# Moving a group's score broadcast and sum into its own step, in the attention stage of a graph-attention and expert kernel

## The chip, the core and the metric

The kernel runs on one core of a Trainium2 chip. The metric is the device time of one execution in microseconds (us), the median of several runs. One execution was also recorded by the hardware profiler; all rows below are from that execution.

## The reference

There are 128 graphs of 128 nodes with 256 features. Everything is float32. Cut to what matters:

```python
def gnn(h, adj, W, a):                       # h = layernorm(x)
    Wh = einsum('bnd,df->bnf', h, W)
    s1 = Wh @ a[:256, 0];  s2 = Wh @ a[256:, 0]
    e = s1[:, :, None] + s2[:, None, :]
    e = where(e > 0, e, 0.2 * e) + log(adj + 1e-6)
    return einsum('bij,bjf->bif', softmax(e, axis=-1), Wh)

x = x + gnn(layernorm(x), adj, W, a)
x = x + ffn(layernorm(x), ...)   # 8 experts, three 256x256 products each, two batch norms,
                                 # gates from a softmax of the mean over graphs
```

## The kernel before

The program has two parts. The first, about 335 of the 2493 us, is the attention stage, and only this one is touched. The second, the experts, needs the gates, which need the mean over all graphs, so it starts when the first part is over.

The attention stage takes the graphs in 32 groups of 4. It is a pipeline written out by hand: each engine has its own program, a function `step(g, layer)` that `over_groups` calls for g = -2 to 33, and an engine handles several groups in one step. In step g TensorE (PE) handles group g (projection), group g-2 (attention output) and group g+1 (transposes of its normalised rows). ScalarE (ACT), VectorE (DVE) and GpSimd (POOL) do likewise. Nothing but semaphores ties the engines together. Within an engine the order is that of the code, so an instruction that waits holds up everything behind it. Steps 6 to 21 also load and split the first weights of the experts (`layer == 1`), steps 22 to 29 the second (`layer == 2`); they run in loops.

The names, with the line of the profile for each, for group g:

- `x_sb` (L327, load by SyncE, SP), two buffers: the load for group g+2 waits until group g has been normalised. `st1`, `mv1` (DVE L572, L586): its statistics. `rstd1`, `nb1` (POOL L404, L407).
- `xn` (ACT L501, `normalise`): the normalised rows, one buffer. `ps_xT` (PE L782) and `xnT` (ACT L554): their transposes in PSUM and in SBUF, one buffer each.
- `ps_wide` (PE L731, `project`): `xnT` times `gw`, 258 columns: the projected rows and the two score columns. `wh` (ACT L550): their copy, two buffers by the parity of g. The copy of group g waits for `h_ready` of group g-2, whose product reads the same buffer.
- `ps_s` (PE L750): the second score of each node, broadcast over the partitions. `s_sb` (ACT L518): the sum with the first score. `l_sb` (DVE L611): the leaky slope. `neg_m` (DVE L616): minus the row maximum. `e_sb` (ACT L529): the exponential. `p_sb` (DVE L680): times `adj` + 1e-6. `rowsum` (DVE L687).
- `ps_pT` (PE L743), `pT` (ACT L511): the transpose of `p_sb`. `ps_h` (PE L769): `pT` times `wh`. It lies in the same banks as `ps_xT` (both are called `ps_th` in the profile). `x1` (DVE L665, called `h` or `w_bc` there): `ps_h` / rowsum + x.
- `acc` (DVE L636 for the lower half of a group, POOL L449 and L453 for the upper, called `resb`): the sum over graphs. `wq_hi` and `w_hi` (ACT L541, L545), `wq_lo` and `w_lo` (POOL L471, L476): the split of the experts' weights.

In the code `a` is group g-1, `b` group g-2, `nxt` group g+1 (on DVE and POOL group g+2), `t` group g-3 and `h` group g-4. `wait(eng, sem, n)` waits for n signals and does nothing for n <= 0; a group signals each of its semaphores once.

Of the kernel before, what the change touches and what calls it, by code (L numbers as in the profile page):

```python
# [21 lines left out]
ACT = mybir.ActivationFunctionType  # L22
AX_X = mybir.AxisListType.X

P = 128
# [6 lines left out]
def wait(eng, sem, value):  # L32

    if isinstance(value, int) and value <= 0:
        return
    eng.wait_ge(sem, value)


def adj_ffn(nc, x, adj, gnn_w, gnn_a, wr, br, w1, b1, g1, be1, m1, v1, w2, b2, g2, be2, m2, v2, wo, bo, out):
    B, N, D = x.shape  # L40
    E = wr.shape[1]
    C = D // P
    GB = 4
    T = GB * N
    G = B // GB
# [11 lines left out]
    with ExitStack() as ctx:  # L57
# [7 lines left out]
        ident = sb("ident", [P, P])  # L65
# [12 lines left out]
        mean_all = sb("mean_all", [P, G, GB])  # L78
# [106 lines left out]
        with ExitStack() as sa:  # L185
# [24 lines left out]
            xnT = sba("xnT", [P, C, T])  # L210
# [77 lines left out]
            def num(g):  # L288
                return 2 * g[0] + g[1]

            def ago(g, n):

                q = g[1] - n
                return (g[0] + q // 2, q % 2)

            def exists(g):
                return not isinstance(g[0], int) or 0 <= num(g) < G
# [12 lines left out]
            def is_step(g, n):  # L310

                return isinstance(g[0], int) and num(g) == n
# [172 lines left out]
            @block.scalar  # L485
            def _(act):

                act.wait_ge(proj_T, 1)
                nc.scalar.activation(gwT[:, :, :], ps_h[:, 0:C, :], ACT.Copy)
                nc.scalar.activation(a_cols[:, :], ps_s[:, 0, 0:2 * C], ACT.Copy).then_inc(proj_T_copied, 1)  # L490
                act.wait_ge(va_ready, 1)
                nc.scalar.activation(gw[:, :, D:D + 2], ps_s[:, 1, 0:2 * C].rearrange("p (c k) -> p c k", k=2),
                                     ACT.Copy).then_inc(va_copied, 1)

                def normalise(g):

                    p = g[1]
                    act.wait_ge(nb1_done, num(g) + 1)
                    wait(act, xnT_ready, num(g))
                    for b4 in range(GB):  # L500
                        last = nc.scalar.activation(xn[:, b4, :], x_sb[p][:, b4, :], ACT.Identity,  # L501
                                                    bias=nb1[p][:, b4:b4 + 1], scale=rstd1[p][:, b4:b4 + 1])
                    last.then_inc(xn_done, 1)

                def step(g, layer):
                    p = g[1]
                    b = ago(g, 2)
                    if exists(b):
                        act.wait_ge(pT_ready, num(b) + 1)
                        wait(act, h_ready, num(b))  # L510
                        nc.scalar.activation(pT[:, :, :], ps_pT[:, :, :], ACT.Copy).then_inc(pT_copied, 1)  # L511
                    a = ago(g, 1)
                    if exists(a):
                        r = a[1]
                        act.wait_ge(s2b_ready, num(a) + 1)
                        wait(act, l_done, num(a))
                        for b4 in range(GB):
                            last = nc.scalar.activation(s_sb[:, b4, :], ps_s[:, b4, :], ACT.Identity,  # L518
                                                        bias=wh[r][:, b4, D:D + 1])
                        last.then_inc(s_done, 1)  # L520
                    nxt = ago(g, -1)
                    if exists(nxt):
                        normalise(nxt)
                    if exists(a):
                        act.wait_ge(neg_m_done, num(a) + 1)
                        wait(act, p_done, num(a))

                        for b4 in range(GB):
                            last = nc.scalar.activation(e_sb[:, b4, :], l_sb[:, b4, :], ACT.Exp,  # L529
                                                        bias=neg_m[:, b4:b4 + 1])  # L530
                        last.then_inc(e_done, 1)
                    if is_step(g, BN_STEP - 1):
                        act.wait_ge(bn_T, 1)
                        nc.scalar.activation(bn_in[:, :, :, :].rearrange("p l i k -> p (l i) k"), ps_bn,
                                             ACT.Copy).then_inc(bn_copied, 1)
                    if is_step(g, G):
                        tile_copy(act, 0, ps_x0)
                    if layer == 1 and p == 1:
                        e = g[0] - K0
                        act.wait_ge(wq_sum, 4 * (e + 1))  # L540
                        nc.scalar.activation(wq_hi[:, e, :, :], w_stage[:, 0:Q, :], ACT.Copy).then_inc(wq_hi_done, 1)  # L541
                    if layer == 2:
                        i = second(g)
                        act.wait_ge(w2_loaded[p], 16 * (g[0] - K1 + 1))
                        nc.scalar.activation(w_hi[:, i, :, :].rearrange("p c n -> p (c n)"),  # L545
                                             w_half[p], ACT.Copy).then_inc(w_hi_done, 1)
                    if exists(g):
                        act.wait_ge(wh_ready, num(g) + 1)
                        wait(act, h_ready, num(g) - 1)
                        nc.scalar.activation(wh[p][:, :, :], ps_wide[:, :, 0:D + 2], ACT.Copy).then_inc(wh_copied, 1)  # L550
                    if exists(nxt):
                        act.wait_ge(xnT_ready, num(nxt) + 1)
                        wait(act, wh_ready, num(nxt))
                        nc.scalar.activation(xnT[:, :, :], ps_xT, ACT.Copy).then_inc(xnT_copied, 1)  # L554
                    t = ago(g, 3)
                    if exists(t) and not is_step(t, G - 1):
                        act.wait_ge(stats2_done, num(t) + 1)
                        nc.scalar.activation(mean_all[:, num(t), :], mv2[t[1]][:, :, 0],
                                             ACT.Copy).then_inc(mean2_done, 1)

                over_groups(act, step)
                for group in range(3):
                    tile_high(act, 0, group)

            @block.vector
            def _(dve):
# [27 lines left out]
                def step(g, layer):  # L594
# [5 lines left out]
                    def stats_part(b4):  # L600

                        if exists(nxt):
                            stats_1(nxt, b4)

                    if exists(a):

                        stats_part(0)
                        stats_part(1)
                        dve.wait_ge(s_done, num(a) + 1)
                        wait(dve, e_done, num(a))  # L610
                        nc.vector.scalar_tensor_tensor(out=l_sb[:, :, :], in0=s_sb[:, :, :], scalar=SLOPE,  # L611
                                                       in1=s_sb[:, :, :], op0=ALU.mult,
                                                       op1=ALU.max).then_inc(l_done, 1)
                        stats_part(2)
                        dve.wait_ge(l_done, num(a) + 1)
                        nc.vector.tensor_reduce(neg_m[:, :], l_sb[:, :, :], AX_X, ALU.max,  # L616
                                                negate=True).then_inc(neg_m_done, 1)
                        stats_part(3)
                    else:
                        for b4 in range(GB):  # L620
                            stats_part(b4)
# [88 lines left out]
            def _(pe):  # L710
# [22 lines left out]
                    return mm  # L733

                def step(g, layer):
                    a = ago(g, 1)
                    b = ago(g, 2)
                    nxt = ago(g, -1)
                    if exists(b):
# [2 lines left out]
                        for b4 in range(GB):  # L742
                            last = nc.tensor.transpose(ps_pT[:, b4, :], p_sb[:, b4, :], ident[:, :])  # L743
                        last.then_inc(pT_ready, 1)
                    if exists(a):

                        pe.wait_ge(wh_copied, num(a) + 1)
                        wait(pe, s_done, num(a))
                        for b4 in range(GB):
                            last = nc.tensor.matmul(ps_s[:, b4, :], wh[a[1]][:, b4, D + 1:D + 2].to_broadcast([P, P]),  # L750
                                                    ident[:, :], start=True, stop=True)
                        last.then_inc(s2b_ready, 1)
                    if is_step(g, G):
                        pe.wait_ge(wh_copied, G)
                        tile_transpose(pe, 0, ps_x0)
# [2 lines left out]
                    if exists(g):  # L758
                        pe.wait_ge(xnT_copied, num(g) + 1)
                        wait(pe, wh_copied, num(g))  # L760
                        project(g, range(GB // 2))
                    if exists(b):

                        pe.wait_ge(pT_copied, num(b) + 1)
# [7 lines left out]
                                last.then_inc(h_low_ready, 1)  # L772
                        last.then_inc(h_ready, 1)
                    if exists(g):
                        project(g, range(GB // 2, GB)).then_inc(wh_ready, 1)
                    if exists(nxt):
                        pe.wait_ge(xn_done, num(nxt) + 1)
                        wait(pe, xnT_copied, num(nxt))
# [507 lines left out]
```

## Time and profile before

| | us |
|---|---|
| time, median of 3 runs | 2492.35 (2492.15 to 2494.12) |
| time of the profiled execution | 2494.85 |
| its span | 2493.1 |
| attention stage | about 0 to 335 |
| first product of the experts' part starts | 348.92 |
| TensorE busy, whole span | 2409.5 (97%) |
| VectorE busy | 1728.2 (69%) |
| ScalarE busy | 1643.7 (66%) |
| GpSimd busy | 458.9 (18%) |

The shares are means over two stages with different limits. The slices of the page show it: TensorE reads 7 and 8 tenths in the first five slices (62 us each) and 9 in all that follow. The chain that ended last lies on TensorE for 85% of the span, on lines of the experts' part. "Idle before" is how long an engine stood still before an instruction, and behind the arrow stands what ended it.

### The profile page before, as it was taken

Reading aid. Unit: us, or ns where it says so; the run is one execution under the profiler, and the core shown is the slowest. Engines: PE = TensorE matmul, PEld = TensorE weight load, DVE = VectorE, ACT = ScalarE, POOL = GpSimd, SP = SyncE. Lnnn points to the kernel's source line nnn. Section 1 sums busy time; section 2 is a strip of 40 time slices with the busy share of each in tenths; the row PEclk is TensorE's granted clock in tenths of the full one; section 3 lists DMA queues with packets and bytes.
Section 4 is the critical chain, followed back from the end, with each engine's and each line's share of the span. In section 5 each row is a group of like instructions: output and inputs, shape, how many; then the busy total and the mean of one; then the engine's idle time right before and its main releaser. Section 6 shows DMA issues by size and latency. Waiting matters only on the chain.

```text
span 2493.1 us, 45081 instructions
## 1 busy us (share of the span) xinstructions
PE 2409.5 (97%) x16304; PEld 2217.6 (89%) x16304; DVE 1728.2 (69%) x2444; ACT 1643.7 (66%) x2497; POOL 458.9 (18%) x487
## 2 busy tenths in 40 slices
PE   7888869999999999999999999999999999999999
PEld 6767658999999999999999999999999999999998
DVE  6888866666666666666666666666666666666665
ACT  6777746666666666666666666666666666666665
POOL 4666632111111100110111111111111100110110
PEclk9999979999999999999999999999999999999999
DMA  5666620000000000000000000000000000000000
GB/s 183 199 189 195 206 89 26 27 26 25 25 25 25 25 25 25 25 17 25 17 17 25 25 25 25 25 25 25 25 25 25 25 25 25 25 17 19 15 17 26
DMA packets 91178, 116.16 MB, mean 47 GB/s; under 512 B 4700, under 2 KB 78856, under 8 KB 91144
## 3 DMA queue, kind: packets, MB, share of 16 engines
q1 hardware_dynamic: 91144, 115.73, 14.4%
q8 instruction: 19, 0.31, 0.1%
q14 instruction: 15, 0.12, 0.0%
HBM read 82.16 MB, written 33.55 MB: 46 GB/s over the span
## 4 chain that ended last, share of the span: by engine, by line
PE 85%; DVE 1%; ACT 0%; issue 0%; ACTq 0%; DVEq 0%
PE ps_y L1186 29%; PE ps_wide L171 29%; PE ps_wide L1168 26%; PE ps_t L132 1%; DVE h_lo L1073 0%; PE ps_y L1234 0%; DVE h L1080 0%; DVE z L1066 0%; ACT h_hi L975 0%; DVE feat_sum L1106 0%; DVE x1t L124 0%; ACT v L980 0%; DVE resb L179 0%; DVE z L1056 0%; DVE h_lo L1088 0%
## 5 line engine op out<-in xcount | busy, mean ns | idle before, releaser
L980 ACT ACTIVATE v<-ps_wide,bn_cols 128x256 f32<-128x256 f32 x768 | 434.7, 566 | 398.6 <-PE ps_wide L1168 271.5
L988 ACT ACTIVATE h<-ps_wide,bn_cols 128x512 f32<-128x512 f32 x512 | 399.2, 780 | 327.2 <-PE ps_wide L171 327.2
L1186 PE MATMUL ps_y<-wo_lo,h_hi 128*128 128x256 f32 x2048 | 578.8, 283 | 0.0
L1186 PE MATMUL ps_y<-wo_hi,h_hi 128*128 128x256 f32 x2048 | 577.2, 282 | 1.6 <-DVE h_lo L1088 1.6
L1186 PE MATMUL ps_y<-wo_hi,h_lo 128*128 128x256 f32 x2048 | 578.3, 282 | 0.0
L1168 PE MATMUL ps_wide<-xq_hi,wq_hi 128*128 128x256 f32 x1792 | 505.6, 282 | 13.8 <-PEq L185 8.4
L1168 PE MATMUL ps_wide<-xq_lo,wq_hi 128*128 128x256 f32 x1792 | 509.2, 284 | 0.0
L1168 PE MATMUL ps_wide<-xq_hi,wq_lo 128*128 128x256 f32 x1792 | 506.5, 283 | 0.0
L1088 DVE TENSOR_TENSOR h_lo<-h,h_hi 128x1024 fp32r<-128x1024 f32 x256 | 318.3, 1243 | 241.9 <-ACT h_hi L994 241.9
L1066 DVE SCALAR_TENSOR_TENSOR z<-ps_wide,bn_cols,v 128x512 f32<-128x512 f32 x256 | 192.2, 751 | 318.2 <-PE ps_wide L1168 318.2
L171 PE MATMUL ps_wide<-h_hi,w_hi 128*128 128x512 f32 x1024 | 404.2, 395 | 2.1 <-DVE h_lo L1073 2.1
L171 PE MATMUL ps_wide<-h_lo,w_hi 128*128 128x512 f32 x1024 | 405.7, 396 | 0.0
L171 PE MATMUL ps_wide<-h_hi,w_lo 128*128 128x512 f32 x1024 | 405.4, 396 | 0.0
L1073 DVE SCALAR_TENSOR_TENSOR h_lo<-z,h_hi 128x1024 fp32r<-128x1024 f32 x256 | 315.8, 1234 | 117.4 <-ACT h_hi L975 117.4
L1186 PEld LDWEIGHTS ps_y<-wo_hi,h_hi 128*128 128x128 f32 x2048 | 386.5, 189 | 1.9 <-DVE h_lo L1088 1.8
L1186 PEld LDWEIGHTS ps_y<-wo_hi,h_lo 128*128 128x128 f32 x2048 | 387.4, 189 | 0.0
L1186 PEld LDWEIGHTS ps_y<-wo_lo,h_hi 128*128 128x128 f32 x2048 | 386.5, 189 | 0.1
L958 POOL TENSOR_TENSOR resb<-resb,bias_out 128x1024 f32<-128x1024 f32 x32 | 85.9, 2685 | 1534.3 <-DMA resb<-x_scratch 1534.3
L1168 PEld LDWEIGHTS ps_wide<-xq_hi,wq_hi 128*128 128x128 f32 x1792 | 340.7, 190 | 26.7 <-issue 9.4
L1168 PEld LDWEIGHTS ps_wide<-xq_hi,wq_lo 128*128 128x128 f32 x1792 | 338.0, 189 | 10.0
L1168 PEld LDWEIGHTS ps_wide<-xq_lo,wq_hi 128*128 128x128 f32 x1792 | 339.5, 189 | 0.0
L1080 DVE TENSOR_TENSOR h<-h,w_bc 128x1024 f32<-128x1024 f32 x256 | 313.8, 1226 | 7.8 <-ACT w_bc L1022 4.9
(131 smaller groups left out, 3141.5 us busy)
## 6 DMA issues: line engine op xcount, KB each, us to landing
x_sb<-in_x SPq DMA_DIRECT2D x32, 512.0 KB, 3.5
res<-in_x SPq DMA_DIRECT2D x32, 512.0 KB, 4.5
x1t<-x_scratch SPq DMA_DIRECT2D x32, 512.0 KB, 3.2
resb<-x_scratch SPq DMA_DIRECT2D x32, 512.0 KB, 3.3
out<-resb SPq DMA_DIRECT2D x32, 512.0 KB, 3.0
adj_sb<-in_adj SPq DMA_DIRECT2D x32, 256.0 KB, 4.7
x_scratch<-h SPq DMA_DIRECT2D x16, 512.0 KB, 3.2
x_scratch<-w_bc SPq DMA_DIRECT2D x16, 512.0 KB, 3.1
```

What stands on the lines that cost most here:

```text
L132: last = nc.tensor.transpose(ps_x[:, c, b4 * N:(b4 + 1) * N], x1t[:, b4, c * P:(c + 1) * P], ident[:, :])
L171: mm = nc.tensor.matmul(acc_ps, w[:, i, c, cols], s[:, c, :], start=start and n == 0, stop=stop and n == len(terms) - 1)
L958: nc.gpsimd.tensor_tensor(resb[:, :, :], resb[:, :, :], bias_out[:, None, :].to_broadcast([P, GB, D]), ALU.add).then_inc(resb_done, 1)
L980: nc.scalar.activation(v[:, slot, :], ps_l1[:, 0, 0:H], ACT.Identity, bias=bn_cols[:, 1, cols], scale=bn_cols[:, 0, cols]).then_inc(done, 1)
L988: nc.scalar.activation(h2[:, m, :], ps_l2[:, m, :], ACT.Relu, bias=bn_cols[:, 3, cols], scale=bn_cols[:, 2, cols]).then_inc(r2_done, 1)
L1066: nc.vector.scalar_tensor_tensor(out=z[:, 0, :], in0=ps_l1[:, 1, :], scalar=bn_cols[:, 0, C * e:C * e + 1], in1=v[:, 0:2, :].rearrange("p ...
L1073: nc.vector.scalar_tensor_tensor(out=h1_lo[:, :, :], in0=z[:, :, :], scalar=0.0, in1=h1_hi[:, :, :].bitcast(F32), op0=ALU.max, op1=ALU.sub ...
L1080: nc.vector.tensor_tensor(h2w[:, :, :].rearrange("p c (b n) -> p (c b) n", n=N), h2[:, :, :].rearrange("p c (b n) -> p (c b) n", n=N), w_b ...
L1088: nc.vector.tensor_tensor(h2_lo[p][:, :, :], h2w[:, :, :], h2_hi[p][:, :, :].bitcast(F32), ALU.subtract).then_inc(lo2_done, 1)
L1168: mm = nc.tensor.matmul(out_ps, w[:, e, q, :], x[:, q, :], start=start and n == 0, stop=stop and n == len(terms) - 1, skip_group_check=True)
L1186: mm = nc.tensor.matmul(ps_y[:, b4, :], h[:, c, cols], w[:, e, c, :], start=(e == 0 and k == 0 and b4 % per_bank == 0), stop=(e == E - 1 a ...
```

## The change

On TensorE `ps_s` is computed for group g at the end of its own step, behind the attention output of group g-2, where it was computed one step later, behind the transposes of `p_sb`. The projection is issued in one piece of all four graphs, where it was issued in two halves around the attention output. On ScalarE `s_sb` is computed for group g in its own step too, behind the next group's `normalise`; the exponential and the copy of the projected rows `wh` now stand ahead of `normalise`, and the weights' split behind the copy of the transposes `xnT`. On VectorE one of the four statistics instructions that stood ahead of `l_sb` and one of those behind it move down by a place. No instruction is added or removed; GpSimd's and SyncE's code is the same.

```diff
@@ ScalarE, step(g, layer)
                     a = ago(g, 1)
                     if exists(a):
-                        r = a[1]
-                        act.wait_ge(s2b_ready, num(a) + 1)
-                        wait(act, l_done, num(a))
-                        for b4 in range(GB):
-                            last = nc.scalar.activation(s_sb[:, b4, :], ps_s[:, b4, :], ACT.Identity,
-                                                        bias=wh[r][:, b4, D:D + 1])
-                        last.then_inc(s_done, 1)
-                    nxt = ago(g, -1)
-                    if exists(nxt):
-                        normalise(nxt)
-                    if exists(a):
                         act.wait_ge(neg_m_done, num(a) + 1)
                         wait(act, p_done, num(a))
...
                         last.then_inc(e_done, 1)
+                    if exists(g):
+                        act.wait_ge(wh_ready, num(g) + 1)
+                        wait(act, h_ready, num(g) - 1)
+                        nc.scalar.activation(wh[p][:, :, :], ps_wide[:, :, 0:D + 2], ACT.Copy).then_inc(wh_copied, 1)
+                    nxt = ago(g, -1)
+                    if exists(nxt):
+                        normalise(nxt)
+                    if exists(g):
+                        act.wait_ge(s2b_ready, num(g) + 1)
+                        wait(act, l_done, num(g))
+                        for b4 in range(GB):
+                            last = nc.scalar.activation(s_sb[:, b4, :], ps_s[:, b4, :], ACT.Identity,
+                                                        bias=wh[p][:, b4, D:D + 1])
+                        last.then_inc(s_done, 1)
...
+                    if exists(nxt):
+                        act.wait_ge(xnT_ready, num(nxt) + 1)
+                        wait(act, wh_ready, num(nxt))
+                        nc.scalar.activation(xnT[:, :, :], ps_xT, ACT.Copy).then_inc(xnT_copied, 1)
+                    t = ago(g, 3)
+                    if exists(t) and not is_step(t, G - 1):
+                        act.wait_ge(stats2_done, num(t) + 1)
...
                         nc.scalar.activation(w_hi[:, i, :, :].rearrange("p c n -> p (c n)"),
                                              w_half[p], ACT.Copy).then_inc(w_hi_done, 1)
-                    if exists(g):
-                        act.wait_ge(wh_ready, num(g) + 1)
-                        wait(act, h_ready, num(g) - 1)
...
-                    if exists(nxt):
-                        act.wait_ge(xnT_ready, num(nxt) + 1)
-                        wait(act, wh_ready, num(nxt))
...
@@ VectorE, step(g, layer)
                         stats_part(0)
-                        stats_part(1)
                         dve.wait_ge(s_done, num(a) + 1)
                         wait(dve, e_done, num(a))
...
-                        stats_part(2)
+                        stats_part(1)
                         dve.wait_ge(l_done, num(a) + 1)
                         nc.vector.tensor_reduce(neg_m[:, :], l_sb[:, :, :], AX_X, ALU.max,
                                                 negate=True).then_inc(neg_m_done, 1)
+                        stats_part(2)
                         stats_part(3)
@@ TensorE, step(g, layer)
                         last.then_inc(pT_ready, 1)
-                    if exists(a):
-
-                        pe.wait_ge(wh_copied, num(a) + 1)
-                        wait(pe, s_done, num(a))
-                        for b4 in range(GB):
-                            last = nc.tensor.matmul(ps_s[:, b4, :], wh[a[1]][:, b4, D + 1:D + 2].to_broadcast([P, P]),
-                                                    ident[:, :], start=True, stop=True)
-                        last.then_inc(s2b_ready, 1)
...
                         wait(pe, wh_copied, num(g))
-                        project(g, range(GB // 2))
+                        project(g, range(GB)).then_inc(wh_ready, 1)
                     if exists(b):
...
                         last.then_inc(h_ready, 1)
                     if exists(g):
-                        project(g, range(GB // 2, GB)).then_inc(wh_ready, 1)
+
+                        pe.wait_ge(wh_copied, num(g) + 1)
+                        wait(pe, s_done, num(g))
+                        for b4 in range(GB):
+                            last = nc.tensor.matmul(ps_s[:, b4, :], wh[g[1]][:, b4, D + 1:D + 2].to_broadcast([P, P]),
+                                                    ident[:, :], start=True, stop=True)
+                        last.then_inc(s2b_ready, 1)
```

TensorE's order in one step inside the loops, with what each instruction waits for, before:

```order
90 L743 MATMUL ps_pT<-ident,p_sb 128x128 [waits pT_copied,p_done]
92 L750 MATMUL ps_s<-ident,wh 128x128 [waits s_done,wh_copied]
94 L731 MATMUL ps_wide<-gw,xnT 128x258 [waits wh_copied,xnT_copied]
95 L731 MATMUL ps_wide<-gw,xnT 128x258 x3
96 L769 MATMUL ps_th<-wh,pT 128x256 [waits x1_done,xnT_copied,wh_copied,pT_copied]
98 L731 MATMUL ps_wide<-gw,xnT 128x258 x4
```

The same step after the change:

```order
87 L741 MATMUL ps_pT<-ident,p_sb 128x128 [waits pT_copied,p_done]
89 L730 MATMUL ps_wide<-gw,xnT 128x258 [waits wh_copied,xnT_copied]
90 L730 MATMUL ps_wide<-gw,xnT 128x258 x7
91 L759 MATMUL ps_th<-wh,pT 128x256 [waits x1_done,xnT_copied,wh_copied,pT_copied]
93 L769 MATMUL ps_s<-ident,wh 128x128 [waits s_done,wh_copied]
96 L778 MATMUL ps_th<-ident,xn 128x128 [waits x1_low_done,xnT_copied,xn_done]
```

The transposes of the next group (`ps_th<-ident,xn`) now stand behind `ps_s`, which waits for `wh_copied` of the same step.

ScalarE's order in a step of the second loop (`layer == 2`), before:

```order
116 L511 ACTIVATE pT<-ps_pT 128x512 [waits h_ready,pT_ready]
117 L518 ACTIVATE s_sb<-ps_s,wh 128x128 [waits l_done,s2b_ready]
120 L501 ACTIVATE xn<-x_sb,nb_0,rstd_0 128x256 [waits xnT_ready,nb1_done]
122 L529 ACTIVATE e_sb<-l_sb,neg_m 128x128 [waits p_done,neg_m_done]
125 L545 ACTIVATE w_hi<-w_stage 128x512
126 L550 ACTIVATE wh<-ps_wide 128x1032 [waits h_ready,wh_ready]
127 L554 ACTIVATE xnT<-ps_th 128x1024 [waits wh_ready,xnT_ready]
```

The same step after the change:

```order
118 L511 ACTIVATE pT<-ps_pT 128x512 [waits h_ready,pT_ready]
119 L518 ACTIVATE e_sb<-l_sb,neg_m 128x128 [waits p_done,neg_m_done]
121 L524 ACTIVATE wh<-ps_wide 128x1032 [waits h_ready,wh_ready]
123 L501 ACTIVATE xn<-x_sb,nb_0,rstd_0 128x256 [waits xnT_ready,nb1_done]
125 L532 ACTIVATE s_sb<-ps_s,wh 128x128 [waits l_done,s2b_ready]
127 L542 ACTIVATE xnT<-ps_th 128x1024 [waits wh_ready,xnT_ready]
131 L557 ACTIVATE w_hi<-w_stage 128x512
```

`normalise` (`xn`) moved from ahead of the exponential and of `wh` to behind both.

## Rows read from the trace of the kernel before

**Rows 1.** Windows: stretch; length; busy of PE, PEld, DVE, ACT, POOL; PEclk, DMA, GB/s
```profile
0.00:62.00 62.00, 49.33 (x258) 41.78 (x259) 38.03 (x130) 41.28 (x91) 27.69 (x56) 1.00 0.59 182
62.00:125.00 63.00, 53.96 (x285) 44.71 (x284) 55.89 (x170) 46.98 (x104) 43.63 (x68) 0.95 0.65 199
...
187.00:249.00 62.00, 52.62 (x268) 43.58 (x267) 54.94 (x164) 44.99 (x101) 42.19 (x62) 0.92 0.63 195
```

**Rows 2.** Waits, 60 to 310 us: who waited for whom, us in total, times, longest
```profile
ACT xnT L554 <- PE ps_th L782: 28.4, 24, 2.3
DVE l_sb L611 <- ACT s_sb L518: 24.8, 24, 2.0
```

**Rows 3.** Line L611 alone: ns min/median/max, and what its engine waited for before it
```profile
L611 DVE SCALAR_TENSOR_TENSOR l_sb<-s_sb x32: 691/886/2477, 25.6 to 329.3; 128x512 f32<-128x512 f32 x32
...
  ACT s_sb L518: 34.7, 32
```

**Rows 4.** Timeline, two steps inside the first loop: start, us, engine, line, operation
```profile
199.96 2.08 ACT L501 ACTIVATE xn<-x_sb,nb,rstd 128x256 f32<-128x256 f32 x4
...
202.06 1.28 ACT L529 ACTIVATE e_sb<-l_sb,neg_m 128x128 f32<-128x128 f32 x4
202.22 0.37 SPq L327 DMA_DIRECT2D x_sb<-in_x  x1
...
203.25 0.93 ACT L541 ACTIVATE wq_hi<-w_stage 128x896 f32 x1
...
205.65 1.01 POOL L443 TENSOR_TENSOR rstd_all<-ve,minus_half 128x4 f32 x1 [0.18 <-POOL ve L440]
205.78 0.67 DVE L680 SCALAR_TENSOR_TENSOR p_sb<-adj_sb,e_sb 128x512 f32<-128x512 f32 x1
...
207.90 1.91 PE L731 MATMUL ps_wide<-gw,xnT 128*128 128x258 f32 x8
...
209.19 2.10 POOL L471 TENSOR_TENSOR wq_lo<-w_stage,wq_hi 128x896 f32 x1
209.36 2.47 DVE L611 SCALAR_TENSOR_TENSOR l_sb<-s_sb 128x512 f32<-128x512 f32 x1 [0.67 <-ACT s_sb L518]
...
209.64 1.89 PE L769 MATMUL ps_th<-wh,pT 128*128 128x256 f32 x8
...
211.37 1.90 PE L731 MATMUL ps_wide<-gw,xnT 128*128 128x258 f32 x8
```

**Rows 5.** Timeline, the first steps of the stage
```profile
9.35 2.06 ACT L501 ACTIVATE xn<-x_sb,nb,rstd 128x256 f32<-128x256 f32 x4
...
11.46 1.97 PE L782 MATMUL ps_th<-ident,xn 128*128 128x128 f32 x8 [2.22 <-ACT xn L501]
...
14.84 1.02 ACT L554 ACTIVATE xnT<-ps_th 128x1024 f32<-128x1024 f32 x1
...
16.00 6.13 PE L731 MATMUL ps_wide<-gw,xnT 128*128 128x258 f32 x16 [1.40 <-ACT xnT L554]
...
22.18 1.03 ACT L550 ACTIVATE wh<-ps_wide 128x1032 f32<-128x1032 f32 x1 [4.36 <-PE ps_wide L731]
23.10 1.02 ACT L554 ACTIVATE xnT<-ps_th 128x1024 f32<-128x1024 f32 x1
...
24.25 3.67 PE L731 MATMUL ps_wide<-gw,xnT 128*128 128x258 f32 x16
...
26.24 0.42 DVE L572 BATCH_NORM_STATS2 st<-x_sb 128x6 f32<-128x256 f32 x1
26.57 0.67 DVE L616 TENSOR_REDUCE neg_m<-l_sb 128x4 f32<-128x512 f32 x1
...
27.77 1.03 PE L782 MATMUL ps_th<-ident,xn 128*128 128x128 f32 x8
```

**Rows 6.** Timeline, the projection of the last group
```profile
318.18 1.91 PE L731 MATMUL ps_wide<-gw,xnT 128*128 128x258 f32 x8
```

**Rows 7.** Tile x_sb: from issue to landing of its 32 loads
```profile
DMA to landing us min/median/max: 3.4/3.5/4.9
```

More of the change, by code:

```diff
@@ L535, in step @@
                                              ACT.Copy).then_inc(bn_copied, 1)
+                    if exists(nxt):
[5 more added lines that the diff above has]
+                        act.wait_ge(stats2_done, num(t) + 1)
+                        nc.scalar.activation(mean_all[:, num(t), :], mv2[t[1]][:, :, 0],
+                                             ACT.Copy).then_inc(mean2_done, 1)
                     if is_step(g, G):
@@ L546, in step @@
                                              w_half[p], ACT.Copy).then_inc(w_hi_done, 1)
-                    if exists(g):
-                        act.wait_ge(wh_ready, num(g) + 1)
-                        wait(act, h_ready, num(g) - 1)
-                        nc.scalar.activation(wh[p][:, :, :], ps_wide[:, :, 0:D + 2], ACT.Copy).then_inc(wh_copied, 1)
-                    if exists(nxt):
-                        act.wait_ge(xnT_ready, num(nxt) + 1)
-                        wait(act, wh_ready, num(nxt))
[L554 to L559, printed above, removed]
                 over_groups(act, step)
@@ L735, in step @@
                 def step(g, layer):
-                    a = ago(g, 1)
                     b = ago(g, 2)
```

## The prediction

> **What bounds the kernel now.** I read the page first, for which part of the span the change touches: the attention stage, the first 335 of 2493.1 us. There TensorE is busy 7 and 8 tenths, behind it 9, so the shares over the whole span say nothing about this stage. Then the windows of the stage [rows 1]. No engine is full: in 187 to 249 us VectorE is busy 54.94 of 62 us, TensorE 52.62, ScalarE 44.99. TensorE's clock is granted at 1.00 in the first 62 us and at 0.95 and 0.92 later, so it is at the lower of its two levels for 10 to 16% of that time. A stage in which two engines are nearly full and none is full is set by rounds: a chain that leaves an engine and comes back to it one step later. The waits [rows 2] show the round of now. VectorE stands before `l_sb` until `s_sb` is there, 24.8 us in 24 steps; over the whole stage 34.7 us in 32 [rows 3], 1.08 us a step. ScalarE waits longer, 28.4 us in 24 steps, for the transposes behind `xnT`, but it has slack: it is busy 45 of 62 us. So VectorE's order sets the end of a step: it works, and stands only from `p_sb` over two products of TensorE and the sum on ScalarE to `l_sb`.
>
> A step's length comes from the projection of group 1 at 24.25 [rows 5] and of group 31 at 318.18 [rows 6]: 293.93 us in 30 steps, 9.80 us each.
>
> **The change, part by part.** No instruction is added or dropped, so the busy times stay, about, and only rounds move. The durations are from rows 4 and 5.
>
> *The wait of VectorE before `l_sb`.* The sum is now formed one step earlier. This wait goes, worth up to 34.7 us if nothing else is late.
>
> *The new round.* The projection is in one piece, so its signal `wh_ready` comes when all four graphs are through. Behind it TensorE does the attention output `ps_h` of group g-2. The copy `wh` of group g waits for both, since `ps_h` reads the buffer that the copy overwrites. That wait was there before, but the second half of the projection stood behind `ps_h` and covered it. `normalise` is now queued behind this copy on ScalarE, the transposes of the next group wait for `normalise`, the copy `xnT` for the transposes, and the next projection for that copy. Each link waits for the one before, and the last starts the first. In numbers, at the full clock:
> - projection, 16 rows of the profile: eight start-to-start are 209.64 - 207.90 = 1.74, so 3.48 [rows 4]
> - `ps_h` to its end: 1.89 [rows 4]
> - TensorE to ScalarE: 16.00 + 6.13 = 22.13 to 22.18, 0.05 [rows 5]
> - `wh` to the start of what follows it: 23.10 - 22.18 = 0.92 [rows 5]
> - `normalise`: 2.08 [rows 4]
> - ScalarE to TensorE: 9.35 + 2.06 = 11.41 to 11.46, 0.05 [rows 5]
> - transposes: 1.03, the row at 27.77 [rows 5]
> - to ScalarE: 0.05, and `xnT` 1.02 [rows 5]
> - `xnT` to the projection: 14.84 + 1.02 = 15.86 to 16.00, 0.14 [rows 5]
>
> Sum 10.71 us, against 9.80. `ps_s` lies beside `normalise`, `s_sb` beside the transposes (2.08 against about 1.1 of TensorE, then 1.14 of ScalarE, as long as the transposes): free but for 0.1. The transposes of `p_sb` lie beside `xnT`. In 30 steps: 30 x 0.91 = +27.3 us. VectorE's work, 54.94 of 62 us or some 9 us a step, fits into 10.71; the removed wait turns into waiting elsewhere, and the gain is nothing.
>
> *The start.* Before, `wh` of group 0 at 22.18 was followed by `xnT` of group 1 at 23.10 and its projection at 24.25. Now behind `wh`, at 23.10, come `normalise` (2.08), the transposes (1.03), `xnT` (1.02) and three hops (0.24): 27.47. That is +3.2 us.
>
> *The clock.* The 9.80 holds its share at the lower level, the 10.71 none. At 10 to 16% of some 340 us, 35 to 54 us lie at the lower level. TensorE's part of the round is 3.48 + 1.89 + 1.03 = 6.4 of 10.71, 60%, and runs at half speed there, so that a us at that level loses 0.3 us: 10 to 16. But the level fell behind pauses of TensorE, and the new round has several short pauses (about 1 us before `ps_s`, 1 before the transposes, 1 before the projection) in place of a long one. Bounds: 0 (it never falls) to +16. I take +8.
>
> *The loads of `x_sb`.* SyncE issues the load of group g+2 when `normalise` of group g is done. That is later now, and VectorE's first statistics instruction in a step, ahead of `l_sb`, needs this load. This is a second round: end of `normalise` to issue 202.22 - 202.04 = 0.18 [rows 4]; landing 3.5 [rows 7]; statistics 26.57 - 26.24 = 0.33 [rows 5]; `l_sb` 0.69 [rows 3]; statistics 0.33; `neg_m` 0.67 [rows 5]; exponential 203.25 - 202.06 = 1.19 [rows 4]; `wh` 0.92; `normalise` 2.08: 9.9, with hops about 10.0. It stays 0.7 below the first round, which is little. In the first loop SyncE also issues two weight loads ahead of every second load of x, and `l_sb` may be held (below), so I add 2 us, between 0 and +9.
>
> *`l_sb` beside GpSimd.* At 209.36 it took 2.47 us where its shortest is 0.691: it started 0.17 after `wq_lo` on GpSimd, 2.10 long, and ended 0.54 after it [rows 3, 4]. It now comes at another place of GpSimd's order, behind `acc`'s upper half and near the weights' split. Held by the same instruction it costs up to 1.8 us in the second round, 0.7 of it covered. The Trainium skill has a rule here (SBUF — State Buffer, section "SBUF: two separate sides"): a VectorE operation with two SBUF inputs and a GpSimd operation that reads SBUF exclude each other for the whole instruction, and the one that starts second waits. The trace agrees for `l_sb` beside `wq_lo` and not for `p_sb`: at 205.78 it ran 0.13 behind the start of a 1.01 us operation of GpSimd on four elements and took 0.67 [rows 4]. By the rule `p_sb` could be up to 0.9 longer where it meets that operation; by the row nothing, and the sum goes by the row.
>
> *The rest.* The weights' split now stands ahead of `pT`: 0.93 us at most [rows 4], under the 3.48 of the projection that precedes `ps_h`. The exponential ahead of `wh` starts when `neg_m` is done, and queued behind it are `wh`, `normalise` and all of the first round: that is the second round, priced above. The statistics that moved on VectorE: zero.
>
> *Sum*, against the profiled execution's 2494.85 (span 2493.1): +27.3 + 3.2 + 8 + 2 = +40.5, so 2535.3. That execution lies 2.5 above the median of 2492.35; the median afterwards should be about 2533.
>
> **The rivals.**
> 1. *VectorE stays the bound, and its wait is simply gone (faster).* For it: 34.7 us of wait [rows 3], and VectorE the fullest engine. Against it: the new round. It decides from the point where the copy `wh` need not wait for `ps_h`: the round is then 10.71 - 1.89 = 8.8, and VectorE's step 9.80 - 1.08 = 8.7. Time: 2492.35 - 30 x 1.0 = about 2462. I give 4%, since the wait on `h_ready` stands in the code with the value of the same step.
> 2. *The load of x ends last.* For it: only 0.7 us of slack, the store, the `res` and the `adj` loads are now issued right behind it, and landings of up to 4.9 were seen [rows 7]. Against it: the load is first in the queue. At 4.9 the round is 11.4, +21 us over the forecast; with `l_sb` held in eight steps instead, +9. Time 2542 to 2554, say 2549. 12%.
> 3. *The clock falls far more often.* If 40% of the stage lay at the lower level: 340 x 0.4 x 0.3 = 41 in place of 8. Time 2566. For it: TensorE idles a fifth of each round now. Against: the pauses are short. 6%.
> 4. *No change.* The round would have to shorten by 0.9 a step, through an overlap that I don't see. Time 2492. 3%.
>
> **How the numbers follow.** The forecast, 2533, gets 75%. Its own range: low with the clock and the loads at nothing, and the round 0.15 shorter, 2492 + 27 + 3 - 5 = 2517; high with both at their upper bound, 2548. Rival 2 lies mostly inside up to 2553. Out of the range are left rivals 1, 3, 4 and the tail of 2, some 15%. Range 2516 to 2553. By over 0.2% (5 us, what a measurement here can tell from no change): faster 4%, within 3%, slower 93%.
>
> **What would show it.** Right: steps of 10.5 to 11 us, the same length throughout the stage; no wait of `l_sb` for `s_sb`; before `wh` ScalarE waits for `ps_h`, not for the projection; TensorE waits before `ps_s` for `wh`, before the transposes for `xn` and before the projection for `xnT`; the experts' part starts some 40 us later and is as long as before. `l_sb`'s first release by the load of x in most steps would speak for rival 2, a granted clock under 0.9 in the windows for rival 3. Wrong: steps under 10 us, or VectorE without pauses.

## The result and the profile after

| | before | after |
|---|---|---|
| time, median of 5 runs | 2492.35 us (2491.86 to 2494.12) | 2536.80 us (2536.0 to 2537.45) |
| span of the profiled execution, us | 2493.1 | 2535.5 |
| projection of group 1 starts | 24.25 | 27.95 |
| projection of group 31 starts | 318.18 | 361.52 |
| a step between them | 9.80 | 11.12 |
| experts' part starts | 348.92 | 390.19 |

The ratio is 1.0177, 95% interval [1.0163, 1.0191]: 44 us slower; 2533 was forecast. The span grew by 42.4 us: +3.7 at the start, 30 x 1.32 = +39.6 in the steps, -2.1 from the last projection to the experts' part and +1.1 in the experts' part, which is as long as before to 0.05%.

One step of the changed kernel, its timeline, as in [rows 4] (start, us, engine, line, operation; in brackets how long the engine stood and what ended it):

```profile
206.43 3.75 PE L730 MATMUL ps_wide<-gw,xnT 128*128 128x258 f32 x16 [0.68 <-ACT xnT L542]
...
208.39 0.43 DVE L571 BATCH_NORM_STATS2 st<-x_sb 128x6 f32<-128x256 f32 x1 [2.17 <-DMA x_sb<-in_x]
208.73 0.67 DVE L609 SCALAR_TENSOR_TENSOR l_sb<-s_sb 128x512 f32<-128x512 f32 x1
...
210.02 1.89 PE L759 MATMUL ps_th<-wh,pT 128*128 128x256 f32 x8
...
210.36 1.28 ACT L518 ACTIVATE e_sb<-l_sb,neg_m 128x128 f32<-128x128 f32 x4 [3.41 <-DVE neg_m L614]
...
212.01 1.03 ACT L524 ACTIVATE wh<-ps_wide 128x1032 f32<-128x1032 f32 x1 [0.36 <-PE ps_th L759]
...
212.93 2.06 ACT L501 ACTIVATE xn<-x_sb,nb,rstd 128x256 f32<-128x256 f32 x4
213.09 1.16 PE L769 MATMUL ps_s<-ident,wh 128*128 128x128 f32 x8 [1.18 <-ACT wh L524]
...
215.05 1.09 PE L778 MATMUL ps_th<-ident,xn 128*128 128x128 f32 x8 [0.80 <-ACT xn L501]
215.18 0.37 SPq L327 DMA_DIRECT2D x_sb<-in_x  x1
...
216.18 1.02 ACT L542 ACTIVATE xnT<-ps_th 128x1024 f32<-128x1024 f32 x1 [0.16 <-PE ps_th L778]
```

Read it as a ladder. The projection starts at 206.43; 3.59 later `ps_h`; 1.99 after that `wh` on ScalarE, released by `ps_h` (0.36 us of waiting); 0.92 later `normalise`; 2.12 later the transposes; 1.13 later `xnT`; and 1.07 after its start, at 217.25, the next projection. The sum is 10.82 us and the next projection starts 10.82 after the last. TensorE stands three times, 0.68, 1.18 and 0.80 us, and each time a ScalarE instruction of this ladder ends it.

This step is one of the shortest, and the steps are not all alike: 12 of the 30 take 10.76 to 10.87 us, the others up to 11.96. Two things lengthen them. In seven pairs of steps and the first one TensorE's clock falls to the lower level (below). And in eight steps of the first loop, every second one, GpSimd holds `l_sb`, the exponential ends later, and `wh` follows the exponential and not `ps_h`:

```profile
218.33 2.08 POOL L471 TENSOR_TENSOR wq_lo<-w_stage,wq_hi 128x896 f32 x1 [0.48 <-ACT wq_hi L553]
219.41 1.55 DVE L609 SCALAR_TENSOR_TENSOR l_sb<-s_sb 128x512 f32<-128x512 f32 x1
...
220.85 1.89 PE L759 MATMUL ps_th<-wh,pT 128*128 128x256 f32 x8
...
221.92 1.28 ACT L518 ACTIVATE e_sb<-l_sb,neg_m 128x128 f32<-128x128 f32 x4 [3.30 <-DVE neg_m L614]
...
223.10 1.00 ACT L524 ACTIVATE wh<-ps_wide 128x1032 f32<-128x1032 f32 x1
```

That step starts at 217.25, its `wh` 5.85 later in place of 5.58, and it is 11.09 long. Where the clock doesn't fall all such steps are 11.08 or 11.09.

The waits of 60 to 340 us, as in [rows 2]: who waited for whom, us in total, times, longest.

```profile
POOL ve L400 <- DVE mv L585: 86.8, 25, 7.1
ACT e_sb L518 <- DVE neg_m L614: 79.7, 25, 4.4
DVE st L571 <- DMA x_sb<-in_x: 64.4, 25, 4.2
...
PE ps_s L769 <- ACT wh L524: 30.7, 25, 1.4
...
PE ps_th L778 <- ACT xn L501: 20.1, 25, 0.8
PE ps_wide L730 <- ACT xnT L542: 14.7, 26, 0.7
ACT wh L524 <- PE ps_th L759: 9.8, 16, 1.4
```

`l_sb`, which waited 34.7 us for `s_sb` [rows 3], waits 0.5 us now, once:

```profile
L609 DVE SCALAR_TENSOR_TENSOR l_sb<-s_sb x32: 673/675/2389, 30.0 to 370.6; 128x512 f32<-128x512 f32 x32
...
  ACT s_sb L532: 0.5, 1
```

In its place VectorE waits for the load of x, 99.6 us in 32 steps, where it was 17.3 us in 5. And that load takes longer to land than in [rows 7]:

```profile
  DMA x_sb<-in_x: 99.6, 32
...
DMA to landing us min/median/max: 3.5/3.9/5.6
```

The three longest waits of the list are those of engines with slack. How little their length says shows in the load's 64.4 us: cutting its round alone won 5.5 us (below). The ladder's own waits are the short ones at the end.

### The profile page after: what moved, and what is told of

Same layout as the page of the kernel before. It is cut to its first block, busy times and chain, and to the rows that moved or that the text cites. A ratio compares the mean times of both kernels' runs of the same rounds, so it can differ in the third digit from the quotient of the medians.

```text
span 2535.5 us, 45093 instructions
## 1 busy us (share of the span) xinstructions
PE 2412.7 (95%) x16304; PEld 2218.3 (87%) x16304; DVE 1717.1 (68%) x2444; ACT 1638.9 (65%) x2497; POOL 459.4 (18%) x487
## 4 chain that ended last, share of the span: by engine, by line
PE 83%; DVE 1%; ACT 0%; issue 0%; ACTq 0%; DVEq 0%
PE ps_y L1182 29%; PE ps_wide L171 28%; PE ps_wide L1164 25%; PE ps_t L132 1%; DVE h_lo L1069 0%; DVE h L1076 0%; PE ps_y L1230 0%; DVE z L1062 0%; DVE x1t L124 0%; ACT h_hi L971 0%; DVE feat_sum L1102 0%; ACT v L976 0%; DVE resb L179 0%; DVE z L1052 0%; DVE h_lo L1084 0%
```

## The experiments

All times are medians of runs beside the kernel before on the same chip, in us. "Step" is the mean over the 30 steps between the projections of groups 1 and 31.

| kernel | us | ratio to before, 95% interval | step |
|---|---|---|---|
| before | 2492 to 2494 | | 9.80 |
| changed | 2536.8 | 1.0177 [1.0163, 1.0191] | 11.12 |
| projection in halves again | 2536.35 | 1.0173 [1.0156, 1.0190] | 11.08 |
| normalise ahead again | 2497.43 | 1.0017 [1.0007, 1.0026] | 9.88 |
| wh doesn't wait | 2519.52 | 1.0101 [1.0084, 1.0118] | 10.53 |
| first statistics behind l_sb | 2531.28 | 1.0150 [1.0133, 1.0167] | 10.96 |
| both of these | 2490.58 | 0.9994 [0.9984, 1.0003] | 9.59 |
| wh doesn't wait, all statistics behind neg_m | 2477.72 | 0.9932 [0.9915, 0.9949] | 9.14 |
| before, projection in one piece | 2494.54 | 1.0004 [0.9995, 1.0014] | 9.85 |
| ps_s twice | 2531.69 | 1.0152 [1.0135, 1.0169] | 10.98 |
| reordered, one statistics ahead of l_sb | 2468.78 | 0.9899 [0.9882, 0.9915] | 8.96 |
| two ahead | 2463.26 | 0.9875 [0.9859, 0.9892] | 8.78 |
| three ahead | 2462.14 | 0.9870 [0.9853, 0.9886] | 8.81 |

**The projection in one piece.** It was undone in the changed kernel, and done alone in the kernel before.

```diff
-                        project(g, range(GB)).then_inc(wh_ready, 1)
+                        project(g, range(GB // 2))
...
+                        project(g, range(GB // 2, GB)).then_inc(wh_ready, 1)
```

> The changed kernel with the projection in two halves around the attention output again, all else as changed. Theory (the round: projection, attention output, copy wh, normalise, transposes, copy xnT): the same two pieces of TensorE work, 3.5 + 1.9 us, stand ahead of the copy wh in either order, so the step stays at 11.1 us and the time within 3 us of the changed kernel's 2536.8. Rival (the projection in one piece is what costs, since the attention output and with it VectorE's x1 come 1.7 us later): the step falls by up to 1.3 us to that of before, 2500.

> The kernel before with one part of the change: the projection in one piece, ahead of the attention output. Theory: wh is copied behind the attention output in either order, normalise and ps_s are where they were, so the round stays; x1's first half can start 1.7 us later, but VectorE reaches it later than that: within 4 us of the kernel before, 2493. Rival (the one piece costs): 10 us or more over the kernel before.

Measured: 2536.35 and 2494.54, both as the theory had it. This part of the change costs nothing that can be measured. In the changed kernel the order of the two pieces ahead of `wh` doesn't matter, only their sum.

**Normalise ahead of the exponential again.**

```diff
+                    nxt = ago(g, -1)
+                    if exists(nxt):
+                        normalise(nxt)
                     a = ago(g, 1)
                     if exists(a):
                         act.wait_ge(neg_m_done, num(a) + 1)
...
-                    nxt = ago(g, -1)
-                    if exists(nxt):
-                        normalise(nxt)
```

> The changed kernel with ScalarE's normalise put back ahead of the exponential, all else as changed. Theory: normalise leaves the round. What stays is projection 3.6, attention output 2.0 to its signal, wh 1.0, ps_s 1.15 (it stands ahead of the transposes), transposes 1.1, xnT 1.07 = 9.9 us against 10.83, and the load of x is issued 3 us earlier or more, so that its waits go too: a step of 9.8 to 10.0 against 11.12, so 2537 - 30 x 1.2 = 2501, range 2494 to 2508. Rival (the load of x ends last): it gains as much or more, 2485 to 2495, since the load's round is what normalise holds. Rival (one piece and the later x1 cost): no more than 10 us gained, 2527.

Measured: 2497.43, 39 us of the 44 back by this place alone. The step is 9.9 to 10.0 in every case but the first, as summed. In this run the clock stays at its upper level from group 1 to group 31, so the 39 us hold what the clock cost too. Here is what the round has become:

```profile
206.33 1.89 PE L759 MATMUL ps_th<-wh,pT 128*128 128x256 f32 x8
208.32 1.03 ACT L527 ACTIVATE wh<-ps_wide 128x1032 f32<-128x1032 f32 x1 [1.95 <-PE ps_th L759]
209.40 1.16 PE L769 MATMUL ps_s<-ident,wh 128*128 128x128 f32 x8 [1.18 <-ACT wh L527]
210.40 1.04 PE L778 MATMUL ps_th<-ident,xn 128*128 128x128 f32 x8
...
211.61 1.04 ACT L542 ACTIVATE xnT<-ps_th 128x1024 f32<-128x1024 f32 x1
...
212.71 3.75 PE L730 MATMUL ps_wide<-gw,xnT 128*128 128x258 f32 x16 [0.83 <-ACT xnT L542]
...
216.30 1.89 PE L759 MATMUL ps_th<-wh,pT 128*128 128x256 f32 x8
```

From `ps_h` to `ps_h` 9.97 us. The transposes now follow `ps_s` without a wait; `wh` still stands in the round, since `ps_s` needs it and is ahead of the transposes. The wait for the load of x fell from 99.6 us in 32 steps to 16.6 in 5. So `normalise` is in both rounds, that of the ladder and that of the load, and this run alone doesn't tell their shares.

**The two rounds apart.** First the wait of `wh` for `ps_h` was taken out. For this the attention output multiplies a constant tile in place of `wh`: the three kernels that do so leave the projected rows out of that product, so they don't compute the attention. They tell only what the wait costs. The edit:

```diff
                         act.wait_ge(wh_ready, num(g) + 1)
-                        wait(act, h_ready, num(g) - 1)
...
-                            last = nc.tensor.matmul(ps_h[:, b4, :], pT[:, b4, :], wh[b[1]][:, b4, 0:D], start=True,
+                            last = nc.tensor.matmul(ps_h[:, b4, :], pT[:, b4, :], gwT[:, b4 % C, :], start=True,
```

> The changed kernel, but the attention output multiplies pT with a constant tile (the projection's transposed weights) in place of the projected rows wh, so the copy wh no longer waits for it; the product has the same shape and place. Theory: the attention output's 1.9 us leave the first round, 10.83 - 1.9 = 8.9. The second round (end of normalise, issue and landing of the load of x, statistics, l_sb, neg_m, exponential, wh, normalise) is then the longest, 10.0 to 10.6 us: a step of 10.2 to 10.6 and 2537 - 30 x 0.7 = 2516, range 2509 to 2522. Rival (the second round has been the last one in most steps already): no gain, 2530 or more. Rival (neither round, VectorE's own order): 2480.

Then VectorE's `stats_part(0)` was put behind `l_sb`, one line moved:

> The changed kernel with VectorE's first statistics instruction of a step behind l_sb in place of ahead of it, so that l_sb doesn't wait for the load of x (neg_m stands behind it still, one statistics instruction later, as does the rest). Theory: the first round ends last in most steps, so little is gained: 0 to 6 us, 2533. Rival (the load of x ends last): neg_m still waits for the statistics, so the wait shortens by l_sb's 0.6 to 2.3 us; where the load ends last each step shortens by that, 20 us or more, 2517 or less.

Then both together, and last `stats_part(0)` to `(3)` all behind `neg_m`:

> The changed kernel with two edits: the attention output multiplies pT with a constant tile in place of wh (the copy wh no longer waits for it), and VectorE's first statistics instruction stands behind l_sb. Theory: both rounds are shortened, the first to 8.9 us and the second by l_sb and a statistics instruction to about 9.0 to 9.4; VectorE's own work is about 8.5 to 9. A step of 9.0 to 9.4, 2537 - 30 x 1.9 = 2480, range 2473 to 2492. Rival (the rounds are not what sets the step): no more than the single edits' sum.

> The changed kernel, with the attention output on a constant tile in place of wh (the copy wh doesn't wait for it) and all four statistics instructions of the next x behind neg_m. With one of them behind l_sb alone the step was 9.6 us and VectorE still waited for the load of x, 32.9 us in 25 steps. Theory: the load's round (normalise, load, statistics, neg_m, exponential, wh, normalise) is now cut, since neg_m no longer waits for the load; what stays is the first round without the attention output, 8.9, and VectorE's own order, 8.5 to 9.0. A step of 9.0 to 9.2, 2490.6 - 30 x 0.5 = 2475, range 2468 to 2481. Rival (something else held the step at 9.6): 2488 or more.

Measured: -17.3, -5.5, -46.2 and -59.1 us against the changed kernel's median (the kernel before lay between 2492.35 and 2494.2 beside these runs). Cutting the first round alone won 17, cutting the second alone 5.5, and both together 46, twice the single gains' sum. That is how two rounds of nearly the same length show themselves: each hides what the other would give. The first single edit leaves the second round last, at 10.2 to 10.6 in most steps, and at 11.08 in the first loop's steps with `l_sb` held, just what these steps take in the changed kernel. The second leaves the first at 10.8. A part of the 46 is the clock, which falls eight times in the changed kernel, four and six times in the single edits, and never with both. The third run was forecast at 2480 and came at 2490.6, inside its range but 0.4 us a step too long. The wait that is left is VectorE's for the load (60 to 310 us):

```profile
DVE st L570 <- DMA x_sb<-in_x: 32.9, 25, 1.5
```

The second round was still last: only `l_sb`'s 0.6 us had left it, where the expectation took off a statistics instruction too, which still stands ahead of `neg_m`. With all four statistics behind `neg_m` the same row reads

```profile
DVE st L570 <- DMA x_sb<-in_x: 3.8, 10, 1.1
```

and most steps are 9.04, their mean 9.14. With both rounds cut, the changed kernel is faster than the one before. That is no fair race, since it leaves out a product's input and with it a wait; the reordered version below shows the gain with nothing left out.

**The clock.** The granted clock has eight stretches at the lower level, 27 us in all, in the changed kernel between the projections of groups 1 and 31, and ten, 34 us, in the kernel before. The ten stretches that the next expectation gives the changed kernel are two too many. What they cost can be read from the lengths of the steps. The 30 steps are 333.57 us. At 10.82 each they would be 324.6; eight steps with `l_sb` held add some 2.1. The other 6.8 us, by difference, lie in the steps with a low stretch and in those right behind them, some 0.85 us a stretch. To test it, `ps_s` was computed twice, so that TensorE pauses less:

```diff
-                        for b4 in range(GB):
+                        for b4 in [*range(GB), *range(GB)]:
                             last = nc.tensor.matmul(ps_s[:, b4, :], wh[g[1]][:, b4, D + 1:D + 2].to_broadcast([P, P]),
```

> The changed kernel with ps_s computed twice in each step, in the 0.8 us in which TensorE waits for normalise (the second time over the first, the same values). It tells what the clock's lower level costs in the changed kernel, which has ten stretches at that level of 3.4 us each in the stage, behind the pauses of TensorE. Theory: the level falls less often or not at all, and the transposes start 0 to 0.2 us later in each step: with 0.8 us won a stretch, 2537 - 8 + 3 = 2532, range 2527 to 2538. Rival (the lower level costs nothing, since ScalarE sets the round): no gain, 2537 to 2542, whatever the clock does.

Measured: 2531.69, 5.1 us less with 128 matmuls more. Windows of the changed kernel and of this one (columns as in [rows 1]):

```profile
187.00:249.00 62.00, 47.33 (x240) 38.89 (x239) 49.80 (x156) 41.16 (x94) 38.15 (x58) 0.94 0.53 170
```

```profile
187.00:249.00 62.00, 49.94 (x296) 42.33 (x295) 48.45 (x155) 42.37 (x96) 40.95 (x60) 1.00 0.53 171
```

One stretch is left of the eight, in a step of 13.7 us in which the load of x landed only 6.2 us after its issue. So the 5.1 us are what seven stretches cost, less that late load and what the added work delays; that is in line with the 6.8 read from the steps. It is part of the steps' length, and not the cause of the change's loss, since the kernel before has ten stretches.

**A version that beats both.** The idea of the change, scores in their own step, with both rounds kept free: `normalise` ahead of the exponential, `ps_s` behind the transposes, `s_sb` behind `xnT`.

```diff
@@ TensorE: ps_s(g) moves from here
-                    if exists(g):
-                        pe.wait_ge(wh_copied, num(g) + 1)
...
                         last.then_inc(xnT_ready, 1)
+                    if exists(g):
+                        pe.wait_ge(wh_copied, num(g) + 1)
...
@@ ScalarE: s_sb(g) behind xnT, normalise as above
                         nc.scalar.activation(xnT[:, :, :], ps_xT, ACT.Copy).then_inc(xnT_copied, 1)
+                    if exists(g):
+                        act.wait_ge(s2b_ready, num(g) + 1)
...
```

> The scores stay in their own step, but behind the next group's transposes on TensorE and behind the copy xnT on ScalarE, and normalise stands ahead of the exponential. Theory: neither wh nor ps_s nor normalise lies in the first round any more: projection 3.6, attention output 2.0, the rest of x1 on VectorE about 0.6, transposes 1.1 (half of them beside x1), xnT 1.07 = 8.3 to 8.8; TensorE's own work is 8.7. VectorE does not wait for s_sb, which is done a step ahead. A step of 8.8 to 9.2: below the kernel before by 30 x 0.8 = 24 us, 2468, range 2458 to 2480. Rival (VectorE's wait before l_sb was never worth anything before): 2490 or more.

Measured: 2468.78, as forecast. VectorE waits for nothing between 60 and 310 us and is busy 61.08 of 62 us:

```profile
187.00:249.00 62.00, 53.26 (x301) 44.73 (x301) 61.08 (x188) 49.01 (x114) 48.09 (x68) 1.00 0.71 224
```

Part of that is `l_sb` held by GpSimd:

```profile
266.44 1.27 POOL L453 TENSOR_TENSOR resb<-resb,x1s_high 128x512 f32<-128x512 f32 x1
...
266.75 1.50 DVE L609 SCALAR_TENSOR_TENSOR l_sb<-s_sb 128x512 f32<-128x512 f32 x1
```

Then the one statistics instruction that the change had moved behind `l_sb` was put back ahead of it, and one more:

> The reordered kernel (normalise ahead of the exponential, scores behind the transposes and behind xnT) with two statistics instructions ahead of l_sb, as in the kernel before, in place of one. In that kernel VectorE waits for nothing between 60 and 310 us and l_sb is over 1 us long in 26 of 32 steps (1.50 at 266.75, held by GpSimd's acc at 266.44, 1.27 long). Theory: l_sb ends when GpSimd's operation is over, wherever it started, so a statistics instruction put ahead of it fills 0.34 us of the time in which it is held: 26 x 0.34 = 9 us less, 2460, range 2456 to 2466. Rival (the order of independent instructions on a full engine is worth nothing): 2468.

> The same with three statistics instructions ahead of l_sb. Theory: another 0.34 us where l_sb is still held with two ahead, less in the steps where it is not: 2452 to 2460. But GpSimd's next operation, the weights' split, may now be the one it meets (1.27 us, or 2.10 in the first loop, 16 and 8 steps): then up to 0.8 a step more, 2468.

Measured: 2463.26 and 2462.14. The length of `l_sb` in the three (ns min/median/max), one, two and three ahead:

```profile
L609 DVE SCALAR_TENSOR_TENSOR l_sb<-s_sb x32: 669/1512/1636, 24.7 to 301.4; 128x512 f32<-128x512 f32 x32
```

```profile
L610 DVE SCALAR_TENSOR_TENSOR l_sb<-s_sb x32: 670/1174/1634, 25.6 to 296.8; 128x512 f32<-128x512 f32 x32
```

```profile
L611 DVE SCALAR_TENSOR_TENSOR l_sb<-s_sb x32: 669/853/1635, 25.1 to 297.3; 128x512 f32<-128x512 f32 x32
```

The median falls by 0.34 and 0.32 us, each time by the statistics instruction that now fills the time. The first gave 5.5 us where 9 were expected, inside its range. The second gave 1.1, which the spread of the runs doesn't tell from nothing, and 2462.14 lies outside the expected 2452 to 2460.

The traces show where the rest went. From 100.16 to 174 us, eight steps of the first loop, `l_sb` takes 12.2, 9.5 and 6.4 us in the three kernels, but `acc` of the lower half (VectorE, L635) takes 8.4, 10.0 and 10.5. It too reads two tiles in SBUF, and in every second step it meets `wq_lo`. With one statistics instruction ahead of `l_sb`, and with three:

```profile
102.83 2.50 POOL L471 TENSOR_TENSOR wq_lo<-w_stage,wq_hi 128x896 f32 x1
104.88 1.13 DVE L635 SCALAR_TENSOR_TENSOR resb<-h,rstd_all,resb 128x256 f32<-128x256 f32 x2
```

```profile
101.96 2.50 POOL L471 TENSOR_TENSOR wq_lo<-w_stage,wq_hi 128x896 f32 x1
103.48 1.66 DVE L635 SCALAR_TENSOR_TENSOR resb<-h,rstd_all,resb 128x256 f32<-128x256 f32 x2
```

`acc` starts earlier and ends as late: 3.18 us behind the start of `wq_lo` in both. What `l_sb` no longer loses to GpSimd, `acc` loses there. In the third kernel VectorE also waits 2.8 us for the load of x in this window:

```profile
L571 DVE BATCH_NORM_STATS2 st<-x_sb 128x6 f32<-128x256 f32 x32 | 11.9, 414 | 2.8 <-DMA x_sb<-in_x 2.8
```

So the step there is 9.21, 9.08 and 9.28, and in the second loop 9.01, 8.68 and 8.49: the third statistics instruction gains in one loop and loses in the other. The two best versions are 1.3% faster than the kernel before.

## Why the prediction was right

- *The removed wait.* It said up to 34.7 us, and that nothing would be left of it. `l_sb` waits 0.5 us now; the wait moved ahead of the statistics. Right, and the reordered versions show what it was worth where no round takes its place: 24 to 32 us, together with the clock, which never falls between their projections of groups 1 and 31.
- *The new round*, 10.71 us. Measured 10.82. The 16 rows of the projection in one go take 3.59, not 3.48; the other links are within 0.09. Its term is 30 x 1.02 = 30.6 in place of 27.3. The sum was made of the links' durations in the trace before, no link was missing, and leaving `normalise` out of it (9.9 forecast and 9.88 measured) confirms the ladder.
- *The start*, +3.2: measured +3.7.
- *The clock*, +8: some 6.8 by the steps' lengths. Its parts were rougher than the result. It took 35 to 54 us at the lower level, where the record has 34 before and 27 after, and the 8 is the middle between nothing and 16: that it came so near is in part luck.
- *The loads*, +2, for the weight loads and for a held `l_sb`: some 2.1, all of it from `l_sb` held beside `wq_lo` in eight steps. The second round itself was longer than summed, 10.46 in a step without that (10.82 less the 0.36 us for which `wh` still waits for `ps_h`) and not 10.0, since the landing takes 3.9 and not 3.5. So its slack was half of the 0.7 given, and rival 2 was closer than its 12% said: in the eight steps the second round did end last, at 0.27 us each and not at the 1.1 behind the rival's +9.
- *The sum*: +42.4 in the span against +40.5. The round is 3.3 over its term and the start 0.5, the clock 1.2 under; -2.1 and +1.1 behind the last projection were not in the sum. The profiled execution lay 0.5 above the median this time and not 2.5, which makes up the rest of 2536.8 against 2533.
- *`l_sb` beside GpSimd.* In the first loop it took 1.5 to 2.4 us in every second step, where it met `wq_lo`, 8 steps against 13 before. The slack took most of it.
- *The same length throughout the stage*: wrong. The steps are 10.76 to 11.96 long, by the clock and by `l_sb`.
- *The one piece and the weights' split*: nothing, as said; the first was tested, the second was not.
- The rivals: 1 failed at the point named, since `wh` waits for `ps_h`. Its time would not have come even without that wait: the run without it has steps of 10.53 and 2519.52 us, not 8.8 and 2462, because the load's round holds it. 3 is excluded: the clock's mean in the windows is 0.94 and more. 4 is excluded by the time.

## What to carry to other kernels

Before you move an instruction in a pipeline of several engines, write down the chain that starts and ends at the same instruction one step later, add up its links from the trace, and compare the sum with the step: a moved instruction that joins such a chain costs in every step whatever the chain then has over the old step, though no engine is full. An early result (the scores a step ahead) is worth having only if it is queued behind what is in the chain and not ahead of it. Where two chains are nearly equally long, cut both in one run: each alone shows only a fraction of what it is worth. And look at the steps one by one: their mean of 11.12 hid that the round is 10.82, and that the rest has two causes.

## What was new about the hardware

- A 512 KB load landed 0.4 us later in the kernels in which other transfers are issued right behind it, though it is first in the queue: median 3.9 us (3.5 to 5.6) in the changed kernel, where the store and the `res` load are issued 0.4 to 0.7 and 1.0 to 1.3 us later, and 3.5 [rows 7] before, 3.4 with `normalise` early, where the store follows 1.9 us later or more. That the transfers behind it are the cause was not tested apart.
- More work on TensorE shortened the run: 128 more matmuls of the program in its pauses, and the granted clock rose from 0.94 to 1.00 in the window shown, for 5 us less. In the changed kernel each stretch at the lower level stood behind a pause of 1.1 to 2.2 us.
- `l_sb` held by GpSimd ends 0.5 to 0.6 us after GpSimd's operation, whether it started 0.2 or 1.1 us behind it: 2.47 beside `wq_lo` in [rows 4], 1.55 beside the same operation at 219.41, 1.50 beside `acc` (266.44 + 1.27 = 267.71, and 268.25). The Trainium skill (SBUF — State Buffer, "SBUF: two separate sides") says that the operation that starts second waits for the whole length of the first: by that rule, the trace agrees for GpSimd's operations on 128x512 and more. It does not agree for those on four elements: in the changed kernel `p_sb`, which also reads two tiles in SBUF, started during such an operation, 1.0 us long, in 27 steps and took 0.67 to 0.70 us.
